# Audio tower on one core: gates and values of the first stage in quarter pieces, folds of the second stage one step later, attention's last stores waited for in the next stage

## The chip, the cores and the metric

The kernel runs on one core of a Trainium2 chip. The metric is the device time of that core in microseconds, the median of three runs. Lower is better. The engines are called TensorE, VectorE, ScalarE, GpSimd and, for issuing transfers, the sync queue (SP). All five run their own instruction lists and meet through semaphores.

## The reference

Everything is fp32. A tokenizer stage reads x, cut into 3000 tokens of 2560 features (32 sequences x 94, the last one of each padded), and a pre-norm transformer block follows:

```python
x = _rms_norm(x, ln_pre_w)
h = jnp.einsum('btd,hd->bth', x, w1)              # 2560 -> 1024
h = jax.nn.silu(h[..., d:]) * h[..., :d]          # gate * value, 512 wide
y = jnp.einsum('btd,od->bto', h, w2)              # 512 -> 1024
h = _rms_norm(y, ln_post_w)
h = h + attention(_layernorm(h))                  # latent q and kv, rope, causal softmax, wo
h = h + ffn(_layernorm(h))                        # base linear + lora experts, router
```

The change lies in the first line of einsum with its gate and value (stage 1), in the second einsum (stage 2), and in the last transfers of attention (stage 3).

## The kernel before

**Stages.** One launch runs five stages one after another: `tok_up` (the first einsum, gate and value), `tok_down` (the second einsum, post-norm, projections to latents, and four "folds" of attention weights per six tiles), `attention`, the output projection `attn_out`, and the feed-forward. Each stage writes one instruction list per engine. The order within an engine is the order in which the code writes it: there is no scheduler. A transfer of the sync queue is issued when all that the queue has to wait for ahead of it is done, so a wait in SP's list holds all later loads.

**Precision.** An fp32 product is made of three fast passes: an operand is split in a high part (ScalarE, line 596: `t_hi`) and the rest (VectorE, line 670: `t_lo`), and TensorE adds lo x hi, hi x lo and hi x hi (lines 734 to 736).

**Stage 1, `tok_up`.** The product of the 1024 x 2560 weights with the tokens is made with seven products of half-size blocks (`SEVEN`) in place of eight. x's tokens are cut in six blocks `TOKC`, four of 512 columns and two of 480; blocks 2pr and 2pr+1 make pair pr of three. Step s of 210 stands for product i = s // 30, pair pr = (s // 10) % 3 and slice kk = s % 10 of ten slices of the inner dimension. Ten steps, a group, fill the four PSUM tiles of one result. In a step
- SP loads one or two pieces of x (line 464) into six slots `raw`, in some steps pieces of the weights (line 450) into six slots `w_raw`. The load of a weight piece waits until the earlier piece of its slot is split (`s_lo_done`);
- GpSimd adds or subtracts two pieces of x (line 538, into `both`), and two of the weights (line 522);
- ScalarE makes `t_hi` (596) and, of the weights, scaled pieces (567) and `s_hi` (579);
- VectorE makes `s_lo` (633), `t_lo` (670), and takes one PSUM tile of the group before into the results `c_t` (`take`, 651 to 655);
- TensorE runs 12 matmuls of 512 or 480 columns, as soon as `t_lo` of the step is there. Operands of five steps have room (`NT`), so VectorE can be at most five steps ahead.

`c_t` holds per token block c a HIGH half (the gates) and a LOW half (the values), each of four quarters m of 128 x 512. The gates are multiplied with the row's norm (line 697, VectorE), go through Silu on ScalarE (line 617) two steps later, and multiply the values (line 702, VectorE). Each is one operation on all four quarters. The tables `GATE_FIRST` and `VALUE` say in which step. Gates stand at steps 163, 166, 169 (c = 0, 2, 4) and 171, 181, 191 (c = 1, 3, 5), values at 176, 186, 196 (c = 1, 3, 5), 199 and 209 (c = 0, 2); c = 4 is done quarter by quarter after the last step. `STORE` sends a finished block to memory as `g_t` (line 470, 1 MB) eight steps later: in the sync queue behind x's loads of steps 184, 194, 204 and 207, and one behind the last.

**Stage 2, `tok_down`.** 24 tiles of 128 tokens. A pipeline of steps (`run_steps`, `stage(k, m, at, ...)`: at a step, the tile that is `at` steps old): g's parts at distance 0, the product y (line 244) at `D_Y` = 1, the latent product a at 3, turned queries at 4. In step 2 (`CENTRE_AT`) the weights of a are centred (line 1102, VectorE) and scaled in eight pieces by ScalarE (`spread`, line 990), and in step 3 `fold_a` multiplies them (line 1234). Four of each six tiles carry one of 16 folds: two TensorE products q (line 1205), copied out by ScalarE (line 1032), then two wide halves v (line 1213), each copied out (line 1005) before the next may use `ps_f`. SP loads a fold's weights two steps ahead of it. A step's code on each engine:

```python
        D_F = 2
                s = fold(k, m, 0)          # SP: the loads
                s = fold(k, m)             # GpSimd, ScalarE, TensorE: at D_F
```

**Stage 3 to 4.** `attention` stores 128 pieces of its output `o_t` (line 1400) from two tiles in turn, and its SP list ends with a wait for all of these stores. Before that it has loaded the first eight slots of the next stage's input. All engines meet at the end of a stage; `attn_out` loads into `raw` (`OutRaw`, object `ox`), and waits for its first `t_lo` (line 1963).

## Time and profile before

| | us |
|---|---|
| median of 3 runs | 2439.2 (2436.16 to 2441.24) |
| profiled execution | 2439.96 |
| its span, first to last instruction | 2438.3 |
| mean granted TensorE clock | 0.982 |
| `tok_up` | 0 to 600 |
| `tok_down` | 600 to 901 |
| `attention` | 901 to 1584 |
| `attn_out` | 1584 to 2065 |
| feed-forward | 2065 to 2438 |

The rows further down are of this one profiled execution. A timeline row gives the start, the duration (us), engine, line, operation, names and shapes, and in brackets how long the engine was idle before and who ended that. A group row adds up all instructions of a line: busy time, mean ns of one, then idle time before them. In the windows, PEclk is the granted TensorE clock as a share of full speed, and DMA the mean busy share of 16 transfer engines. Step numbers of `tok_up` are found by counting `t_lo` operations: step 162 of TensorE begins at 451.44, step 185 loads x at 514.61.

### The profile page before, as it was taken

How to read it: one execution, taken by the hardware profiler on the slowest of the kernel's cores; microseconds unless marked ns; L12 is line 12 of the kernel's file. 1: busy time of each engine (PE TensorE's matmuls, PEld its weight loads, DVE VectorE, ACT ScalarE, POOL GpSimd, SP SyncE). 2: the span in 40 equal slices, each digit the busy share in tenths (PEclk: the TensorE clock that was granted, in tenths of full speed). 3: DMA queues.
4: the chain of work that ended last, by engine and by line, in shares of the span. 5: the costliest groups of instructions: out<-in, count | busy, mean ns of one | idle time of the engine just before them, and what ended most of it. 6: DMA issues, size and time to landing. Idle time of an engine off the chain costs nothing. (4 is left out here: it accounts for less than half of the span.)

```text
span 2438.3 us, 45823 instructions
## 1 busy us (share of the span) xinstructions
PE 2326.4 (95%) x14640; PEld 2038.1 (84%) x14640; DVE 1811.2 (74%) x3542; ACT 1240.9 (51%) x3724; POOL 1218.7 (50%) x1012
## 2 busy tenths in 40 slices
PE   8999999988899979999999999899999998999998
PEld 6888888866577758999999999788888877899998
DVE  8987777776467758989898989655776575777775
ACT  5566554442355549999999999732332223111110
POOL 5667776673023336677767776510676553111110
PEclk9999999999999989999999999899999999999999
DMA  7774567777466740111111112296888988122121
GB/s 247 242 233 147 180 214 255 241 241 273 147 214 229 229 143 17 57 52 47 51 56 51 45 51 68 69 327 195 241 250 238 290 271 270 53 70 70 69 69 52
DMA packets 319400, 382.00 MB, mean 157 GB/s; under 512 B 23680, under 2 KB 227968, under 8 KB 319104
## 3 DMA queue, kind: packets, MB, share of 16 engines
q1 hardware_dynamic: 311472, 352.30, 45.8%
q0 software_dynamic: 7184, 25.69, 2.7%
q10 hardware_dynamic: 576, 2.10, 0.3%
q8 instruction: 64, 1.05, 0.2%
q14 instruction: 104, 0.85, 0.1%
HBM read 297.68 MB, written 81.80 MB: 156 GB/s over the span
## 5 line engine op out<-in xcount | busy, mean ns | idle before, releaser
L1537 ACT ACTIVATE attn_prob<-attn_prob,attn_bias 94x94 f32<-94x94 f32 x1024 | 366.7, 361 | 45.8 <-DVE attn_bias L1613 44.3
L670 DVE TENSOR_TENSOR up_t_lo<-early_raw,up_t_hi 128x512 fp32r<-128x512 f32 (+1 forms) x210 | 221.0, 1056 | 120.1 <-ACT up_t_hi L596 117.8
L538 POOL TENSOR_TENSOR early_raw<-early_raw 128x512 f32<-128x512 f32 (+1 forms) x150 | 231.9, 1551 | 142.5 <-DMA early_raw<-x_f 82.3
L1658 POOL TENSOR_TENSOR attn_prob<-attn_prob,attn_share 94x752 f32<-94x752 f32 x128 | 188.3, 1471 | 177.5 <-DVE attn_share L1621 177.5
L1913 POOL TENSOR_TENSOR early_raw<-early_raw 128x512 f32<-128x512 f32 x120 | 170.2, 1423 | 199.9 <-DMA early_raw<-o_t 199.5
L1963 DVE TENSOR_TENSOR out_t_lo<-early_raw,out_t_hi 128x512 fp32r<-128x512 f32 x168 | 159.6, 954 | 139.5 <-ACT out_t_hi L1927 138.7
L596 ACT ACTIVATE up_t_hi<-early_raw 128x512 fp32r<-128x512 f32 (+1 forms) x210 | 130.4, 622 | 258.2 <-POOL early_raw L538 179.6
L1927 ACT ACTIVATE out_t_hi<-early_raw 128x512 fp32r<-128x512 f32 x168 | 105.0, 631 | 307.6 <-POOL early_raw L1913 155.9
L734 PE MATMUL up_ps<-up_t_lo,early_s_hi 128*128 128x512 f32 (+1 forms) x616 | 241.1, 391 | 12.8 <-DVE up_t_lo L670 12.8
L735 PE MATMUL up_ps<-up_t_hi,early_s_lo 128*128 128x512 f32 (+1 forms) x616 | 239.1, 388 | 0.0
L736 PE MATMUL up_ps<-up_t_hi,early_s_hi 128*128 128x512 f32 (+1 forms) x616 | 238.9, 388 | 0.0
L2117 POOL TENSOR_TENSOR ffn_res<-shared_k_t,ffn_bias 128x1024 f32<-128x1024 f32 x24 | 58.3, 2429 | 303.1 <-DVE ffn_o L2242 263.1
L1537 ACT ACTIVATION_READ_ACCUMULATOR attn_prob<-attn_prob,attn_bias 94x1 f32 x1024 | 192.5, 188 | 0.0
L1986 PE MATMUL out_ps<-early_s_hi,out_t_lo 128*128 128x512 f32 x384 | 150.3, 392 | 9.4 <-DVE out_t_lo L1963 9.4
L1592 DVE TENSOR_TENSOR attn_prob<-attn_ps_s,attn_mask 94x752 f32<-94x752 f32 x128 | 119.3, 932 | 51.9 <-PE attn_ps_s L1452 51.6
L1987 PE MATMUL out_ps<-early_s_lo,out_t_hi 128*128 128x512 f32 x384 | 150.1, 391 | 0.0
L1988 PE MATMUL out_ps<-early_s_hi,out_t_hi 128*128 128x512 f32 x384 | 150.0, 391 | 0.0
L1649 POOL TENSOR_TENSOR attn_q_a<-attn_by_cos,attn_by_sin 64x376 f32<-64x376 f32 x128 | 144.3, 1127 | 10.6 <-POOL attn_by_sin L1645 1.1
L734 PEld LDWEIGHTS up_ps<-up_t_lo,early_s_hi 128*128 128x128 f32 x616 | 116.7, 189 | 38.0 <-issue 8.7
L244 PE MATMUL ffn_ps_o<-ffn_w_hi,ffn_xt_lo 128*128 128x384 f32 (+1 forms) x576 | 138.8, 346 | 1.2 <-DVE ffn_xt_lo L2206 1.2
L736 PEld LDWEIGHTS up_ps<-up_t_hi,early_s_hi 128*128 128x128 f32 x616 | 116.5, 189 | 22.5
L735 PEld LDWEIGHTS up_ps<-up_t_hi,early_s_lo 128*128 128x128 f32 x616 | 116.6, 189 | 21.8
(267 smaller groups left out, 6628.2 us busy)
## 6 DMA issues: line engine op xcount, KB each, us to landing
early_raw<-o_t SPq DMA_DIRECT2D x288, 256.0 KB, 4.9
early_raw<-x_f SPq DMA_DIRECT2D x240, 256.0 KB, 3.9
shared_ring<-w SPq DMA_DIRECT2D x120, 256.0 KB, 4.0
early_raw<-x_f SPq DMA_DIRECT2D x120, 240.0 KB, 4.0
shared_ring<-wvo SPq DMA_DIRECT2D x96, 256.0 KB, 4.9
o_t<-attn_o_t SPq DMA_DIRECT2D x128, 188.0 KB, 1.9
shared_ring<-wo SPq DMA_DIRECT2D x32, 512.0 KB, 6.7
y<-early_raw POOLq DMA_DIRECT2D x24, 512.0 KB, 3.6
```

Of the source, the lines that this page charges most:

```text
L538: nc.gpsimd.tensor_tensor(both[n % 2][:, 0:w], a, b, SEVEN[i].op_b).then_inc(both_done, 1)
L670: nc.vector.tensor_tensor(t_lo[s % NT][:, 0:w], src, t_hi[s % NT][:, 0:w], ALU.subtract).then_inc(lo_done, 1)
L734: nc.tensor.matmul(o, sh, tl, start=(kk == 0), stop=False)
L735: nc.tensor.matmul(o, sl, th, start=False, stop=False)
L736: last = nc.tensor.matmul(o, sh, th, start=False, stop=(kk == KH - 1))
L1537: last = nc.scalar.activation(prob[u % NPR][0:SEQ, h, part], prob[u % NPR][0:SEQ, h, part], ACT.Exp, bias=bias[u % 2][0:SEQ, n:n + 1], sca ...
L1658: nc.gpsimd.tensor_tensor(p4, p4, share[u % 2][0:SEQ, :].unsqueeze(2).broadcast_to((SEQ, 8, SEQ)), ALU.mult).then_inc(prob_done, 1)
L1913: nc.gpsimd.tensor_tensor(ox.at(s), ox.at(s), ox.at(s, 1), ox.product(s).op_a).then_inc(ox.both_done, 1)
L1963: nc.vector.tensor_tensor(t_lo[s % NT][:], ox.at(s), t_hi[s % NT][:], ALU.subtract).then_inc(ox.lo_done, 1)
L1986: nc.tensor.matmul(ps[g % NB][:], t_lo[s % NT][:, j, :], sh, start=(kk == 0), stop=False)
L1987: nc.tensor.matmul(ps[g % NB][:], t_hi[s % NT][:, j, :], sl, start=False, stop=False)
L1988: last = nc.tensor.matmul(ps[g % NB][:], t_hi[s % NT][:, j, :], sh, start=False, stop=(kk == KB - 1))
```

## The change

Three edits, each on its own.

**Quarters.** Gate, Silu and value work on one quarter (`piece(c, mh, m)`, 128 x 512 or 480) instead of the half. Waits on `taken` are for that quarter alone. New tables give a step for each quarter: gates of c = 0 at steps 162 to 165, c = 2 at 166 to 169, c = 1 at 170, 172, 173, 174, c = 4 at 175, 177, 182, 188, c = 3 at 189, 189, 190, 190, c = 5 at 191, 191, 192, 192. Values: c = 1 at 193, 193, 194, 194, c = 3 at 195 to 198, c = 0 at 199, 199, 200, 200, c = 5 at 201, 201, 202, 202, c = 2 four at 209. The stores follow eight steps behind a block's last value as before: 202, 206, 208 and two behind the last load. Lines of the changed file are 12 to 13 higher from the middle of `tok_up` on.

**Folds.** `D_F` = 3 instead of 2, the load of a fold's weights at distance 1 instead of 0. All engines' fold parts move to one step later.

**Attention.** The wait for the last stores of `o_t` leaves the end of attention's SP list and stands at the start of `attn_out`'s SP list. The tiles `o_t` are placed elsewhere in the stage's memory (moved up behind `w_lo`, not shown), and their semaphores belong to `OutRaw`.

```diff
@@ -414,18 +414,27 @@
         STATS = ps[group(4, 2) % 2][0][:, width(2):width(2) + TILES]
         RATE_AT = STAT_AT + KH + 4
         assert RT * len(TOKC) == TOKP and RT == 4 * P
-        GATE_FIRST, VALUE = {}, {}
-        for pr in range(PAIR):
-            GATE_FIRST[RATE_AT + 9 + 3 * pr] = 2 * pr
-            GATE_FIRST[KH * group(5, pr + 2) + 1] = 2 * pr + 1
-            VALUE[KH * group(5, pr + 2) + 6] = 2 * pr + 1
-            if pr < 2:
-                VALUE[KH * group(6, pr + 1) + 9] = 2 * pr
-        gates = sorted(GATE_FIRST, key=lambda s: s)
-        nth_gate = {GATE_FIRST[s]: n for n, s in enumerate(gates)}
-        values = sorted(VALUE)
-        nth_value = {VALUE[s]: n for n, s in enumerate(values)}
-        STORE = {s + 8: VALUE[s] for s in values}
+        G6, G7 = KH * group(5, 0), KH * group(6, 0)
+        GATE_AT = {0: (G6 + 12, G6 + 13, G6 + 14, G6 + 15), 2: (G6 + 16, G6 + 17, G6 + 18, G6 + 19),
+                   1: (G6 + 20, G6 + 22, G6 + 23, G6 + 24), 4: (G6 + 25, G6 + 27, G7 + 2, G7 + 8),
+                   3: (G7 + 9, G7 + 9, G7 + 10, G7 + 10), 5: (G7 + 11, G7 + 11, G7 + 12, G7 + 12)}
+        VALUE_AT = {1: (G7 + 13, G7 + 13, G7 + 14, G7 + 14), 3: (G7 + 15, G7 + 16, G7 + 17, G7 + 18),
+                    0: (G7 + 19, G7 + 19, G7 + 20, G7 + 20), 5: (G7 + 21, G7 + 21, G7 + 22, G7 + 22),
+                    2: (G7 + 29, G7 + 29, G7 + 29, G7 + 29)}
+        gates = sorted((x, c, m) for c in GATE_AT for m, x in enumerate(GATE_AT[c]))
+        values = sorted((x, c, m) for c in VALUE_AT for m, x in enumerate(VALUE_AT[c]))
+        nth_gate = {(c, m): n for n, (x, c, m) in enumerate(gates)}
+        nth_value = {(c, m): n for n, (x, c, m) in enumerate(values)}
+        STORE = {VALUE_AT[c][-1] + 8: c for c in VALUE_AT}
+        assert len(STORE) == len(VALUE_AT) and min(GATE_AT[0]) >= RATE_AT + 8
+        def gates_of(s):
+            return [(c, m) for x, c, m in gates if x == s]
+        def values_of(s):
+            return [(c, m) for x, c, m in values if x == s]
         def rates(c):
@@ -433,11 +442,15 @@
         def rate(c):
             a, w = TOKC[c]
-            return ssq[:, a:a + w].unsqueeze(1).broadcast_to((P, MB, w))
+            return ssq[:, a:a + w]
         def half(c, mh):
             a, w = TOKC[c]
             return c_t[:, MB * mh:MB * mh + MB, a:a + w]
+        def piece(c, mh, m):
+            a, w = TOKC[c]
+            return c_t[:, MB * mh + m, a:a + w]
         @block.sync
         def _(sp):
@@ -466,7 +479,7 @@
             def store(c):
                 a, w = TOKC[c]
-                sp.wait_ge(g_done, nth_value[c] + 1)
+                sp.wait_ge(g_done, nth_value[c, MB - 1] + 1)
                 sp.dma_start(d["g_t"][:, :, a:a + w], half(c, LOW)).then_inc(g_stored, 16)
             sp.dma_start(fac, d["pre_ln"]).then_inc(fac_in, 16)
@@ -495,7 +508,7 @@
                     for n in range(4):
                         ws.load(sp, n)
                 if s == STEPS - 5:
-                    sp.wait_ge(gate_scaled, len(TOKC))
+                    sp.wait_ge(gate_scaled, MB * len(TOKC))
                     sp.dma_start(k_t[:].rearrange("p (n w) -> p n w", n=KM), d["wa"]).then_inc(wa_in, 16)
             for s in sorted(STORE):
                 if s >= STEPS:
@@ -611,10 +624,9 @@
                     nc.scalar.activation(dst, raw[raws.slot(k)][:, 0:w], ACT.Square).then_inc(sq_done, 1)
                 if s in begins:
                     first_piece(begins[s])
-                if s - 2 in GATE_FIRST:
-                    c = GATE_FIRST[s - 2]
-                    act.wait_ge(gate_scaled, nth_gate[c] + 1)
-                    nc.scalar.activation(half(c, HIGH), half(c, HIGH), ACT.Silu).then_inc(silu_done, 1)
+                for c, m in gates_of(s - 2):
+                    act.wait_ge(gate_scaled, nth_gate[c, m] + 1)
+                    nc.scalar.activation(piece(c, HIGH, m), piece(c, HIGH, m), ACT.Silu).then_inc(silu_done, 1)
         @block.vector
         def _(dve):
@@ -689,17 +701,17 @@
                     nc.vector.tensor_scalar(own, var[:, 0, :], RMS_EPS, None, ALU.mult).then_inc(own_done, 1)
                     dve.wait_ge(pad_set, 1)
                     nc.vector.transpose(r_t, r).then_inc(rate_turned, 1)
-                if s in GATE_FIRST:
-                    c = GATE_FIRST[s]
-                    for n in range(TOKC[c][0] // RT, rates(c)):
-                        dve.wait_ge(rate_in[n], 16)
-                    dve.wait_ge(taken, 4 * last_of[(c // 2, HIGH, c % 2)] + 4)
-                    nc.vector.tensor_tensor(half(c, HIGH), half(c, HIGH), rate(c), ALU.mult).then_inc(gate_scaled, 1)
-                if s in VALUE:
-                    c = VALUE[s]
-                    dve.wait_ge(silu_done, nth_gate[c] + 1)
-                    dve.wait_ge(taken, 4 * last_of[(c // 2, LOW, c % 2)] + 4)
-                    nc.vector.tensor_tensor(half(c, LOW), half(c, LOW), half(c, HIGH), ALU.mult).then_inc(g_done, 1)
+                for c, m in gates_of(s):
+                    if m == 0:
+                        for n in range(TOKC[c][0] // RT, rates(c)):
+                            dve.wait_ge(rate_in[n], 16)
+                    dve.wait_ge(taken, 4 * last_of[(c // 2, HIGH, c % 2)] + m + 1)
+                    nc.vector.tensor_tensor(piece(c, HIGH, m), piece(c, HIGH, m), rate(c), ALU.mult).then_inc(gate_scaled, 1)
+                for c, m in values_of(s):
+                    dve.wait_ge(silu_done, nth_gate[c, m] + 1)
+                    dve.wait_ge(taken, 4 * last_of[(c // 2, LOW, c % 2)] + m + 1)
+                    nc.vector.tensor_tensor(piece(c, LOW, m), piece(c, LOW, m), piece(c, HIGH, m),
+                                            ALU.mult).then_inc(g_done, 1)
             g = NI * PAIR
             a, w = TOKC[4]
             for m in range(MB):
@@ -859,20 +871,20 @@
-        D_F = 2
+        D_F = 3
...
                     if not first(t, 2):
                         sp.wait_ge(key_done, t - 1)
                     sp.dma_start(turns[u % 2][:], d["turns"][t]).then_inc(turns_in[u % 2], 16)
-                s = fold(k, m, 0)
+                s = fold(k, m, 1)
                 if s is not None:
                     p, b, turn = s
                     if not first(p, 2):
@@ -1347,7 +1359,7 @@
         prob_t_done = mem.sem("prob_t_done")
         weighed = mem.sem("weighed")
         o_done = mem.sem("o_done")
-        o_stored = mem.sems("o_stored", 2)
+        o_stored = ox.o_stored
         zeroed = mem.sem("zeroed")
         cleared = mem.sem("cleared")
         table_in = mem.sem("table_in")
@@ -1405,8 +1417,6 @@
                     ox.load(sp, m - 4)
             run_steps(sp, N, DEPTH, U, body, last=1)
-            for b in range(2):
-                sp.wait_ge(o_stored[b], 16 * N // 2)
         @block.tensor
         def _(pe):
@@ -1771,6 +1781,7 @@
         self.all = mem.sb("raw", [P, self.SLOTS, 512])
         self.raw = [self.all[:, i, :].rearrange("p (k n) -> p k n", n=P) for i in range(self.SLOTS)]
         self.raw_in = mem.sems("raw_in", self.SLOTS)
+        self.o_stored = mem.sems("o_stored", 2)
         self.both_done = mem.sem("both_done")
         self.lo_done = mem.sem("lo_done")
         self.steps = 2 * self.PAIR * len(OUT_SEVEN)
@@ -1882,6 +1893,8 @@
                 sp.wait_ge(taken, PAIR * final + pr + 1)
                 sp.dma_start(d["h"][t], c_t[t]).then_inc(lent_stored if t == lent else h_stored, 16)
+            for b in range(2):
+                sp.wait_ge(ox.o_stored[b], 16 * PAIRS * GROUPS // 2)
             for s in range(STEPS):
                 i, pr, half = ox.place(s)
                 if s >= ox.SLOTS:
```

In the listings of order below, a row is one instruction (x and a number: so many alike in a row) with its line, its names and its size; the listings of the changed kernel have its own lines.

VectorE in `tok_up`, before: the value of block 1 (line 702, step 176) among `take`, `s_lo` (633) and `t_lo` (670) of steps 176 to 181; the next row is the gate of block 3 (line 697).

```order
L702 TENSOR_TENSOR up_c_t<-up_c_t 128x4x512
L670 TENSOR_TENSOR up_t_lo<-early_raw,up_t_hi 128x480
L655 TENSOR_TENSOR up_c_t<-up_c_t,up_ps_2 128x512
L633 TENSOR_TENSOR early_s_lo<-shared_ring,early_s_hi 128x512
L670 TENSOR_TENSOR up_t_lo<-early_raw,up_t_hi 128x480
L655 TENSOR_TENSOR up_c_t<-up_c_t,up_ps_3 128x512
L633 TENSOR_TENSOR up_s_lo<-shared_ring,up_s_hi 128x512
L670 TENSOR_TENSOR up_t_lo<-early_raw,up_t_hi 128x480
L633 TENSOR_TENSOR up_s_lo<-shared_ring,up_s_hi 128x512
L670 TENSOR_TENSOR up_t_lo<-early_raw,up_t_hi 128x512
L633 TENSOR_TENSOR up_s_lo<-shared_ring,up_s_hi 128x512
L670 TENSOR_TENSOR up_t_lo<-early_raw,up_t_hi 128x512
```

After, the same stretch of VectorE's list: quarters of block 4's gate (line 709) at steps 177 and 182.

```order
L709 TENSOR_TENSOR up_c_t<-up_c_t,shared_k_t 128x480
L645 TENSOR_TENSOR early_s_lo<-shared_ring,early_s_hi 128x512
L682 TENSOR_TENSOR up_t_lo<-early_raw,up_t_hi 128x480
L667 TENSOR_TENSOR up_c_t<-up_c_t,up_ps_3 128x512
L645 TENSOR_TENSOR up_s_lo<-shared_ring,up_s_hi 128x512
L682 TENSOR_TENSOR up_t_lo<-early_raw,up_t_hi 128x480
L645 TENSOR_TENSOR up_s_lo<-shared_ring,up_s_hi 128x512
L682 TENSOR_TENSOR up_t_lo<-early_raw,up_t_hi 128x512
L645 TENSOR_TENSOR up_s_lo<-shared_ring,up_s_hi 128x512
L682 TENSOR_TENSOR up_t_lo<-early_raw,up_t_hi 128x512 x2
L709 TENSOR_TENSOR up_c_t<-up_c_t,shared_k_t 128x480
L645 TENSOR_TENSOR early_s_lo<-shared_ring,early_s_hi 128x512
```

Between steps 176 and 182 stand two quarters in place of two whole operations.

The sync queue at the end of `tok_up`, before: x's loads (464), stores of `g_t` (470), and the next stages' weights (212, 499). The first store of the list stands ahead of x of step 185.

```order
L470 DMA g_t<-up_c_t 512x1x512
L464 DMA early_raw<-x_f 128x512 x20
L470 DMA g_t<-up_c_t 512x1x512
L464 DMA early_raw<-x_f 128x512 x10
L464 DMA early_raw<-x_f 128x480 x2
L212 DMA shared_ring<-w 128x1024 x4
L464 DMA early_raw<-x_f 128x480 x8
L470 DMA g_t<-up_c_t 512x1x480
L464 DMA early_raw<-x_f 128x480 x2
L499 DMA shared_k_t<-wa 128x3072
L464 DMA early_raw<-x_f 128x480 x4
L470 DMA g_t<-up_c_t 512x1x512
```

After (loads 477, stores 483, weights 212 and 512):

```order
L477 DMA early_raw<-x_f 128x512 x30
L477 DMA early_raw<-x_f 128x480 x2
L212 DMA shared_ring<-w 128x1024 x4
L477 DMA early_raw<-x_f 128x480 x4
L483 DMA g_t<-up_c_t 512x1x512
L477 DMA early_raw<-x_f 128x480 x6
L512 DMA shared_k_t<-wa 128x3072
L477 DMA early_raw<-x_f 128x480 x2
L483 DMA g_t<-up_c_t 512x1x512
L477 DMA early_raw<-x_f 128x480 x4
L483 DMA g_t<-up_c_t 512x1x512
L477 DMA early_raw<-x_f 128x480 x2
```

The 32 loads of x and the four of weights follow one another without a store, and three stores stand ahead of the last 14, the last 6 and the last 2 loads of 480 columns.

TensorE in `tok_down` at the steps 2 and 3, before: fold 0 (1205, 1213) behind y of tile 1, then y of tile 2 with fold 1's first product.

```order
L1205 MATMUL down_ps_f<-down_wk,down_wqn 128x128 x2
L1213 MATMUL down_ps_f<-shared_ring,down_wv 64x512 x4
L244 MATMUL down_ps_y<-early_s_hi,down_g_lo 128x512 x2
L244 MATMUL down_ps_y<-early_s_lo,down_g_hi 128x512 x2
L244 MATMUL down_ps_y<-early_s_hi,down_g_hi 128x512 x2
L244 MATMUL down_ps_y<-early_s_hi,down_g_lo 128x512 x2
L244 MATMUL down_ps_y<-early_s_lo,down_g_hi 128x512 x2
L244 MATMUL down_ps_y<-early_s_hi,down_g_hi 128x512 x2
L1205 MATMUL down_ps_f<-down_wk,down_wqn 128x128 x2
```

After: fold 0 (1217, 1225) behind y of tile 2 (the three rows at the top are the end of it), then `fold_a` (1246) and the first a.

```order
L244 MATMUL down_ps_y<-early_s_hi,down_g_lo 128x512 x2
L244 MATMUL down_ps_y<-early_s_lo,down_g_hi 128x512 x2
L244 MATMUL down_ps_y<-early_s_hi,down_g_hi 128x512 x2
L1217 MATMUL down_ps_f<-down_wk,down_wqn 128x128 x2
L1225 MATMUL down_ps_f<-shared_ring,down_wv 64x512 x2
L1246 MATMUL down_ps_a<-shared_k_t,early_raw 128x384 x32
L244 MATMUL down_ps_a<-down_wga_hi,down_g_lo 128x384
L244 MATMUL down_ps_a<-down_wga_lo,down_g_hi 128x384
```

Fold 0 has moved behind y of tile 2, in step 3, and its two wide halves stand on either side of `fold_a` and a of tile 0.

## Rows read from the trace of the kernel before

**Rows 1.** The page's first part: busy us of each engine, share of the span, instructions.

```profile
PE 2326.4 (95%) x14640; PEld 2038.1 (84%) x14640; DVE 1811.2 (74%) x3542; ACT 1240.9 (51%) x3724; POOL 1218.7 (50%) x1012
```

**Rows 2.** Windows: length, busy PE PEld DVE ACT POOL, PEclk, DMA share, GB/s.

```profile
447.00:491.00 44.00, 44.00 (x200) 37.10 (x199) 35.04 (x28) 24.07 (x31) 33.26 (x19) 1.00 0.74 240
491.00:532.00 41.00, 31.81 (x116) 24.24 (x115) 30.18 (x24) 20.09 (x31) 28.22 (x18) 0.88 0.71 232
560.00:584.00 24.00, 24.00 (x110) 20.44 (x109) 8.78 (x10) 4.24 (x7) 9.26 (x8) 1.00 0.95 345
624.00:638.00 14.00, 8.52 (x27) 4.79 (x26) 7.43 (x21) 8.80 (x18) 2.77 (x4) 0.76 0.30 103
```

**Rows 3.** Timeline of TensorE in stage 1, steps 162 and 189.

```profile
451.44 0.39 PE L734 MATMUL up_ps<-up_t_lo,up_s_hi 128*128 128x512 f32 x1
...
525.23 0.79 PE L734 MATMUL up_ps<-up_t_lo,up_s_hi 128*128 128x512 f32 x1 [4.72 <-DVE up_t_lo L670]
```

**Rows 4.** Groups of GpSimd and VectorE, 447 to 569 us.

```profile
L538 POOL TENSOR_TENSOR early_raw<-early_raw 128x512 f32<-128x512 f32 (+1 forms) x41 | 70.0, 1714 | 38.6 <-DVE up_t_lo L670 20.8 <-DMA early_raw<-x_f 17.8
L522 POOL TENSOR_TENSOR shared_ring<-shared_ring 128x512 f32<-128x512 f32 x10 | 15.2, 1516 | 1.4 <-ACT shared_ring L567 1.3
L670 DVE TENSOR_TENSOR up_t_lo<-early_raw,up_t_hi 128x512 fp32r<-128x512 f32 (+1 forms) x40 | 47.0, 1176 | 27.4 <-ACT up_t_hi L596 26.9
L697 DVE TENSOR_TENSOR up_c_t<-up_c_t,shared_k_t 128x2048 f32<-128x2048 f32 (+1 forms) x6 | 16.4, 2737 | 0.0
L702 DVE TENSOR_TENSOR up_c_t<-up_c_t 128x2048 f32<-128x2048 f32 (+1 forms) x4 | 11.1, 2784 | 0.0
```

**Rows 5.** Timeline of VectorE: one earlier step of stage 1, and step 162.

```profile
104.25 1.21 DVE L670 TENSOR_TENSOR up_t_lo<-early_raw,up_t_hi 128x512 fp32r<-128x512 f32 x1
105.38 0.68 DVE L680 TENSOR_TENSOR shared_k_t<-shared_k_t,shared_ring 128x512 f32<-128x512 f32 x1
105.98 0.65 DVE L651 COPY up_c_t<-up_ps 128x480 f32<-128x480 f32 x1
106.55 1.22 DVE L670 TENSOR_TENSOR up_t_lo<-early_raw,up_t_hi 128x512 fp32r<-128x512 f32 x1
...
446.24 0.69 DVE L670 TENSOR_TENSOR up_t_lo<-early_raw,up_t_hi 128x512 fp32r<-128x512 f32 x1 [0.15 <-ACT up_t_hi L596]
```

**Rows 6.** Timelines of GpSimd and sync queue, and the queue's waits 447 to 569.

```profile
522.14 1.26 POOL L538 TENSOR_TENSOR early_raw<-early_raw 128x512 f32<-128x512 f32 x1 [6.28 <-DMA early_raw<-x_f]
523.36 1.27 POOL L522 TENSOR_TENSOR shared_ring<-shared_ring 128x512 f32<-128x512 f32 x1
...
513.89 0.68 SPq L470 DMA_DIRECT2D g_t<-up_c_t  x1
...
SPq L450 <- DVE early_s_lo L633: 15.8, 4, 6.6
```

**Rows 7.** Timelines of ScalarE, TensorE and VectorE at stage 2's first fold.

```profile
624.92 4.14 ACT L990 ACTIVATE shared_k_t<-shared_k_t,down_post_col 128x384 f32<-128x384 f32 x8
628.96 1.00 ACT L1048 ACTIVATE down_junk<-down_ps_y 128x1024 bf16<-128x1024 f32 x1
...
631.32 1.15 ACT L1059 ACTIVATE early_raw<-down_z,down_vec 128x1024 f32<-128x1024 f32 x1 [0.45 <-DVEq L1145]
...
630.92 1.97 PE L1213 MATMUL down_ps_f<-shared_ring,down_wv 128*64 128x512 f32 x4 [4.76 <-ACT down_wv_out L1005]
...
625.76 1.21 DVE L1135 TENSOR_TENSOR down_z<-down_ps_y,down_post 128x1024 f32<-128x1024 f32 x1
```

**Rows 8.** Timeline of TensorE at the end of stage 2.

```profile
888.17 0.52 PE L1287 MATMUL down_ps_d<-all_ident,down_qk 128*128 128x128 f32 x3 [2.59 <-POOL down_qk L966]
```

**Rows 9.** Timelines of the sync queue and TensorE at attention's end.

```profile
1558.97 23.35 SPq L1400 DMA_DIRECT2D o_t<-attn_o_t  x9
1584.31 0.34 SPq L1877 DMA_DIRECT2D out_c_t<-y  x1
...
1585.75 0.80 PE L1986 MATMUL out_ps<-early_s_hi,out_t_lo 128*128 128x512 f32 x1 [6.75 <-DVE out_t_lo L1963]
```

4 lines of the change are left out of this document (2 added, 2 removed).

## The prediction

> **What bounds the kernel now.** I read the busy shares first: TensorE works 2326.4 of 2438.3 us [rows 1], so the time is TensorE's work plus the 112 us in which it stands, and a change is worth what it takes from those. The windows then say where it stands near the places the change touches. In the first stage it is full until 491, then busy 31.81 of 41 us up to 532, at a mean granted clock of 0.88 [rows 2]. That is 9.2 us of waiting, and 0.12 x 41 = 4.9 us (4.7 without the part that fell into waits) of matmuls at the lower of the two clock levels (1.2 instead of 2.4 GHz); the clock fell after TensorE had stood, as 4.72 us before 525 [rows 3]. Together 13.9 us. In the second stage's start, from 624 to 638, it is busy 8.52 of 14 us at a clock of 0.76: 5.5 us of waiting and 0.24 x 14 = 3.3 us of slow clock [rows 2].
>
> Why it stands at 491 to 532 takes three views. From 447 to 569 (steps 162 to 202) VectorE and GpSimd have nearly the same list of SBUF work to do. A GpSimd add takes 1.22 us when it starts alone (522.14 to 523.36, [rows 6]) and 1.71 in the mean [rows 4]; the t_lo subtraction takes 0.69 alone, or 1.21 when a GpSimd add is running [rows 5]. The two take turns, so their times add up. 51 adds x 1.22 = 62 us; 50 splits (t_lo and s_lo) x 0.60, the distance at which one follows another (105.38 to 105.98 in the pattern of [rows 5]: 2.30 a step holds one add of 1.22, half-hidden, a split, a one-tile operation and a copy) = 30; ten big gates and values x 2.2 = 22. Sum 114 of the 122 us. Into the 8 us left fall the waits of the sync queue: it stood 15.8 us for s_lo [rows 6], and at 513.89 put a 1 MB store of g_t ahead of the loads of x, for which GpSimd then stood 6.28 us [rows 6]. TensorE has to have these 40 steps in 40 x 2.72 = 109 us; it had a lead of 451.44 - 446.93 = 4.5 us at step 162 [rows 3, 5], used it, and stood.
>
> **The change, part by part.**
>
> *Quarters.* Eleven VectorE operations of about 2.75 us (16.4 us for six, 11.1 for four, [rows 4], one later) become 44 of 512 columns, the six Silus 24. Their sum hardly moves: four quarters at the 0.60 pitch are 2.4 us against 2.2, ten sets +2 us. On ScalarE, busy 24.07 of 44 and 20.09 of 41 us [rows 2], the 18 more instructions lie beside other work. So the port floor of steps 162 to 202 is 114 + 2 = 116 us, less the lead of 4.5, against 109: TensorE must still give 2.5 to 3.5 us if nothing overlaps beyond the pitches, none if a few per cent more of it does. What is gained is place: before step 185, where weights are folded on nearly each step, stand 15 quarters instead of six whole operations (24 quarters). Nine quarters x 0.6 to 1.0 = 5.4 to 9 us leave the stretch in which the lead was zero. They come back at steps 188 to 202, with 25 quarters in 15 steps; a step with one such operation and a copy runs in 2.30 us [rows 5], under TensorE's 2.72, one with two in about 2.9, a little over. Ten double steps cost 2 us of lead, the five single ones give 2 back.
>
> *Stores.* The store that stood at step 184 goes to 202, the others to 206, 208 and behind the last load. That frees 1.05 MB / 345 GB/s [rows 2] = 3.0 us in front of x at step 185, and removes most of the 6.28 us of GpSimd. But between steps 202 and 209 now three stores lie ahead of the last load of x instead of two. There the queues are full already (share 0.95, 345 GB/s from 560 to 584, [rows 2]). The extra 1.1 MB are 3.2 us. Since the heavy stretch before is shorter, SP comes to these loads earlier; I charge half, 1.5 us, bounds 0 and 3.2.
>
> Sum of the stage: of 13.9 us I leave 3 for the port floor, 2 for the chain over s_lo that the change does not touch (sync queue to DMA to GpSimd to ScalarE to VectorE), 1.5 for the last loads: **7.4 us gained**. Bounds: 13.9 (all gone) and 0 (the port floor and the stores take it all).
>
> A rule of the Trainium skill speaks against quarters. The trace shows the cost of a short operation as a pitch of 0.60 us in a row of them [rows 5]. The page "VectorE: DVE Perf Modes", section "The TRN2 errata — SBUF-src ops pay a fixed extra latency per instruction", gives an fp32 tensor_tensor (N+151)/0.96 ns, which is 691 ns for 512 columns and 2291 for 2048. By it four quarters would cost 0.47 us more than one whole, ten sets 4.7 us instead of my 2, and the stage would gain 4.7 instead of 7.4 us. The duration of a single one agrees (0.69); the pitch does not, and the sum goes by the pitch.
>
> *Folds.* The distance from load to use stays two steps; both move by one. At step 2 TensorE stood 4.76 us before the second half of fold 0 [rows 7], because ScalarE, between the fold's first and second copy, had to spread eight pieces (4.14 us) and square y [rows 7]. After the change TensorE goes on with y of tile 2 (24 matmuls x 0.23 = 5.5 us, its g_lo is there) up to 629.3 and the fold's first product up to 629.9. ScalarE spreads from 622.5 on, begins y's square when z is there (625.76 + 1.21 = 627.0), needs 631.32 + 1.15 - 628.96 = 3.5 us for y [rows 7], and with the next g_hi and the fold's own copies (1.3 us) is done at 631.9. So TensorE waits 2.1 us where it waited 5.5, and after so little idle I expect no slow clock: 5.5 + 3.3 - 2.1 = **6.7 us gained**; with the slow clock back, 3.4. At the other end the last fold falls to step 25, where TensorE stood 2.59 us for GpSimd [rows 8]: the fold's 2.7 us of matmuls fill that hole and push the last tile by some 2.5 us, while a fold less stands before. That is nil, plus or minus 1. SP is moved past one load of g (tile 2 is loaded ahead of fold 1 now), which only helps. Nothing in the steady part changes.
>
> *Attention's stores.* The last store is issued until 1558.97 + 23.35 = 1582.32, the next stage begins on SP at 1584.31, TensorE at 1585.75 [rows 9]. The 2.0 us between are landing plus the engines' meeting. How they split no row shows; I take 0.4 us for the meeting, which stays, and 1.6 for the landing, since a landing is the longer of the two: **1.6 us gained**, bounds 0 and 2.0. SP itself waits as before, with eight slots of o_t (22 us of matmuls) loaded ahead and nothing else queued behind it but y and weights needed from step 3 and 6 on: at nothing.
>
> Total 7.4 + 6.7 + 1.6 = 15.7 us. The profiled execution took 2439.96 us (span 2438.3), 0.8 over the median of 2439.2: 2439.96 - 15.7 = **2424.3 us**.
>
> **The rivals.**
> 1. *All stalls of the first stage go*: the floor overlaps and the late stores hide. For it: t_lo takes 1176 ns in the mean against 690 alone [rows 4, 5], so operations do run side by side for a part. Against: the pitches hold that part already. 13.9 + 6.7 + 1.6 = 22.2: 2417.8.
> 2. *The stage gains nothing*: VectorE and GpSimd do the same work, the double steps and the stores at the end take back what the place gives. For it the floor of 116 us and share 0.95 at the end; against, the 6.28 us behind one store. 6.7 + 1.6 = 8.3: 2431.7.
> 3. *The fold's wait only moves*: TensorE stands for the fold's first copy as long as it did for the second, and the clock falls. Stage two gains 1: 7.4 + 1 + 1.6 = 10: 2430.
> 4. *Slower: every quarter waits for a GpSimd add.* Stretched from 0.60 to 1.67 us (0.60 and most of an add of 1.22), 40 quarters cost 67 us instead of the 27.5 of [rows 4]: 39 more. VectorE's idle time in the stretch, 27.4 us before t_lo [rows 4], covers as much; 12 us come on top of today's stalls, and 5 of slow clock: 17 - 8.3 = 8.7 slower, 2448.7. It decides where the mean quarter passes (27.5 + 27.4)/40 = 1.37 us. Against it: there are only 51 adds, and each can hold up one operation.
> That the change does not do what it says is open only for attention: if another engine comes last to the meeting, 1.6 less.
>
> **How the numbers follow.** Forecast 0.45 (2419 to 2429), rival 1 0.15, rival 2 0.22, rival 3 0.11, rival 4 0.07. The range of 8 in 10 leaves out most of rival 4 and the far ends of 1: 2416 to 2435. A measurement of this kernel tells about 0.2%, 4.9 us, from no change: under 2434.3 is faster. The forecast and rival 1 lie under it, of rivals 2 and 3 three quarters (their other ends, a slow clock or stores at 3.2 us, cross it): 0.45 + 0.15 + 0.25 = 0.85; within 0.2% 0.09, slower 0.06.
>
> **What would show it.** Right: no TensorE idle over 1.5 us between 447 and 560 and a granted clock of 0.95 or more there; x's loads at step 185 not behind a store; a wait of about 2 us before fold 0's first wide product with the clock at full speed until the stage's end; TensorE's first product of the output stage about 5.2 us after attention's last instead of 6.75. Wrong: TensorE waiting on t_lo in steps 189 to 194 with VectorE busy throughout (the port), or in 205 to 209 with GpSimd waiting on x (the stores), or the half clock in the second stage's first 15 us beyond its start.

## The result, and the profile after

The changed kernel took 2426.31 us, median of 6 runs (2420.08 to 2427.83), beside 2437.18 for the kernel before in 6 runs. The ratio is 0.9948 with a 95% interval of 0.9937 to 0.9959: faster by 12.7 us (10.0 to 15.4). (The two medians themselves differ by 10.9 us; "less" goes by the ratio everywhere below.) Measured again in the experiments below it was 0.9936 (0.9921 to 0.9951), faster by 15.6 us. The forecast was 15.7 us less and the range 2416 to 2435. The profiled execution took 2427.59 us, its span is 2425.9.

The first part of the page answers to [rows 1]. TensorE's busy time is the same to 0.5 us, so of the 12.4 us between the two spans 11.9 are time in which it stands no longer. Matmuls at the slow clock count as busy for longer: what the first stage got back of that (3.4 us, by the measure further down) came in again elsewhere, 1.9 us of it in the second stage.

```profile
PE 2325.9 (96%) x14640; PEld 2038.6 (84%) x14640; DVE 1821.9 (75%) x3575; ACT 1242.8 (51%) x3742; POOL 1205.4 (50%) x1012
```

The windows of [rows 2], now of the changed kernel (length, busy PE, PEld, DVE, ACT, POOL, granted clock, DMA share, GB/s):

```profile
447.00:491.00 44.00, 44.00 (x199) 37.00 (x198) 41.39 (x40) 25.94 (x44) 30.43 (x21) 1.00 0.78 251
491.00:532.00 41.00, 37.86 (x160) 30.34 (x159) 33.08 (x31) 20.74 (x35) 28.48 (x20) 0.96 0.77 250
560.00:584.00 24.00, 23.79 (x109) 19.83 (x107) 12.57 (x17) 5.38 (x9) 11.97 (x9) 1.00 1.01 388
624.00:638.00 14.00, 12.48 (x41) 6.95 (x40) 7.66 (x25) 5.56 (x13) 2.30 (x4) 1.00 0.39 129
```

Between 491 and 532 TensorE is busy 37.86 us instead of 31.81, at a clock of 0.96 instead of 0.88; 44 matmuls more stand in the window. Between 624 and 638 it is busy 12.48 instead of 8.52, at full clock. What is left of [rows 3] between 491 and 532 is in the main one wait, before step 185 as then. (Counted by `t_lo` operations, the row with 4.72 us in [rows 3] is step 185 too, not 189 as its heading has it.)

```profile
514.01 0.50 PE L746 MATMUL up_ps<-up_t_lo,up_s_hi 128*128 128x512 f32 x1 [0.35 <-DVE up_t_lo L682]
519.52 0.79 PE L746 MATMUL up_ps<-up_t_lo,up_s_hi 128*128 128x512 f32 x1 [2.50 <-DVE up_t_lo L682]
```

The groups of VectorE and GpSimd, 449 to 566 us, answer to [rows 4]:

```profile
L682 DVE TENSOR_TENSOR up_t_lo<-early_raw,up_t_hi 128x512 fp32r<-128x512 f32 (+1 forms) x41 | 42.0, 1026 | 10.4 <-ACT up_t_hi L609 9.7
L709 DVE TENSOR_TENSOR up_c_t<-up_c_t,shared_k_t 128x512 f32<-128x512 f32 (+1 forms) x24 | 29.8, 1255 | 0.0
L713 DVE TENSOR_TENSOR up_c_t<-up_c_t 128x512 f32<-128x512 f32 (+1 forms) x16 | 16.7, 1070 | 0.0
...
L551 POOL TENSOR_TENSOR early_raw<-early_raw 128x512 f32<-128x512 f32 (+1 forms) x41 | 59.3, 1449 | 44.1 <-DVE up_t_lo L682 26.1 <-DMA early_raw<-x_f 11.5 <-issue 6.5
```

A quarter of a gate takes 1255 ns in the mean and of a value 1070, where a quarter of the whole was 684 to 696. The 40 quarters are busy 46.5 us instead of 27.5. In return t_lo fell from 1176 to 1026 ns and GpSimd's adds from 1714 to 1449. Whether this comes of the portions or of the new steps the pair of traces cannot tell; the runs under "Size or place" do.

For the account I worked out of each trace the time from a stage's first matmul to its last, the gap to the next stage, and of TensorE's slow clock the sum of (1 - granted clock) x 2 us over windows of 2 us. These are worked out from the timelines, not rows of a view. The last of them also counts slow clock in which TensorE stood, so it is not all time lost. Of this one profiled pair:

| us | before | changed | difference | forecast |
|---|---|---|---|---|
| start to first matmul | 8.7 | 10.0 | +1.3 | 0 |
| `tok_up` | 587.2 | 579.6 | -7.6 | -7.4 |
| gap | 9.6 | 9.9 | +0.2 | 0 |
| `tok_down` | 290.9 | 287.8 | -3.1 | -6.7 |
| `attention` | 678.6 | 679.8 | +1.2 | 0 |
| gap behind attention | 6.75 | 3.18 | -3.6 | -1.6 |
| `attn_out` and feed-forward | | | -0.8 | 0 |

The sum is -12.4. Two of the forecast's differences do not fit, `tok_down` by 3.6 us and the gap by 2.0 the other way, and for both the experiments have more traces of the same code. The change touches neither the start nor the work within `attention`; over fourteen traces these two range from 8.7 to 11.0 and from 677.8 to 680.4 us, so their differences are chance.

### The profile page after: what moved, and what is told of

Its sections match the earlier page's. It is cut to its first block and busy times, and to the rows that moved or that the text cites. A ratio compares the mean times of both kernels' runs of the same rounds, so it can differ in the third digit from the quotient of the medians.

```text
span 2425.9 us, 45879 instructions
## 1 busy us (share of the span) xinstructions
PE 2325.9 (96%) x14640; PEld 2038.6 (84%) x14640; DVE 1821.9 (75%) x3575; ACT 1242.8 (51%) x3742; POOL 1205.4 (50%) x1012
## 5 line engine op out<-in xcount | busy, mean ns | idle before, releaser
L682 DVE TENSOR_TENSOR up_t_lo<-early_raw,up_t_hi 128x512 fp32r<-128x512 f32 (+1 forms) x210 | 224.0, 1070 | 102.1 <-ACT up_t_hi L609 99.7
L551 POOL TENSOR_TENSOR early_raw<-early_raw 128x512 f32<-128x512 f32 (+1 forms) x150 | 220.2, 1471 | 148.8 <-DMA early_raw<-x_f 72.6
L748 PEld LDWEIGHTS up_ps<-up_t_hi,early_s_hi 128*128 128x128 f32 x616 | 116.0, 188 | 22.4
L244 PE MATMUL ffn_ps_o<-ffn_w_lo,ffn_xt_hi 128*128 128x384 f32 (+1 forms) x576 | 134.8, 339 | 0.0
```

The lines of the kernel that those rows point to most:

```text
L244: last = nc.tensor.matmul(o, x, w, start=a, stop=b, skip_group_check=onto)
L551: nc.gpsimd.tensor_tensor(both[n % 2][:, 0:w], a, b, SEVEN[i].op_b).then_inc(both_done, 1)
L682: nc.vector.tensor_tensor(t_lo[s % NT][:, 0:w], src, t_hi[s % NT][:, 0:w], ALU.subtract).then_inc(lo_done, 1)
L748: last = nc.tensor.matmul(o, sh, th, start=False, stop=(kk == KH - 1))
```

## The experiments

Each kernel was timed in five rounds or more beside the kernel before, four kernels together on one chip. "Less" is against the kernel before, worked out from the ratio and its median there (2438.28, 2437.98 and 2438.48 us for the three sets).

### Each part alone

The three edits were applied to the kernel before one by one. Together they are exactly the changed kernel.

The folds:

```diff
-        D_F = 2
+        D_F = 3
...
-                s = fold(k, m, 0)
+                s = fold(k, m, 1)
```

> Only the fold's step is moved (D_F = 3, loads at distance 1); nothing is left out. Prediction: 6.7 us less than before, nearly all in the first 15 us of the second product's stage, with no half clock there. Rival: the changed kernel's trace shows only 3.2 us less between TensorE's first and last matmul of the stage (290.9 before, 287.8 after), because 2.68 us of waiting with half clock stand at 680 where 1.1 us stood before, and the clock falls earlier at the stage's end; then this run gains about 3 us and shows both places.

Measured: ratio 0.996 (0.9947 to 0.9973), 9.8 us less. `tok_down` took 283.4 us, 7.5 less. Of the wait at the first fold 1.16 us are left, and a new one is there, at 689.58, with the clock at 0.56 to 0.58 for four us:

```profile
689.58 1.97 PE L1213 MATMUL down_ps_f<-shared_ring,down_wv 128*64 128x512 f32 x4 [2.61 <-ACT down_wv_out L1005]
```

The changed kernel has it at the same step. So one of the two places that the rival named showed, and its 3 us did not. At the stage's end the two traces differ, though both have nearly the same waits: here TensorE waits 1.67 us before the last fold and keeps its clock,

```profile
876.88 0.68 PE L1205 MATMUL down_ps_f<-down_wk,down_wqn 128*128 128x128 f32 x4 [1.67 <-ACT down_wv_out L1005]
```

```profile
874.00:886.00 12.00, 8.83 (x46) 5.58 (x42) 5.86 (x29) 7.08 (x26) 4.77 (x13) 1.00 0.36 137
```

there it waits 1.77 and the 12 us around it run at 0.72 (timeline, and window of the changed kernel):

```profile
870.46 0.86 PE L1217 MATMUL down_ps_f<-down_wk,down_wqn 128*128 128x128 f32 x4 [1.77 <-ACT down_wv_out L1017]
```

```profile
868.00:880.00 12.00, 9.52 (x36) 6.17 (x35) 4.17 (x23) 5.89 (x21) 3.96 (x9) 0.72 0.36 137
```

The slow clock takes 3.6 us of the stage in one and 9.1 in the other. The 7.5 us of this trace lie within the interval of the 9.8 (6.6 to 12.9), and the trace has other stages that are shorter without a change in them (`attn_out` 461.1 against 464.8).

Attention's stores:

```diff
-            for b in range(2):
-                sp.wait_ge(o_stored[b], 16 * N // 2)
...
+            for b in range(2):
+                sp.wait_ge(ox.o_stored[b], 16 * PAIRS * GROUPS // 2)
```

> Only the wait for attention's last stores is moved; nothing is left out. Prediction: 1.6 us less. The changed kernel's trace has 3.6 us less between attention's last matmul and the next stage's first (6.75 to 3.18), of which 2.3 us is that the last copy of o_t waited 0.70 instead of 2.99 us for an older store: if that belongs to the change, this run gains 3.6 us and its last copy waits under 1 us; if it was chance, 1.3 to 1.6 us and the copy waits differently from run to run.

Measured: 0.9989 (0.998 to 0.9998), 2.7 us less (0.5 to 4.9). The gap behind attention was 3.01 us. In five traces that wait at the old place (the kernel with the folds alone and four more below) it was 4.66, 4.62, 4.66, 4.42 and 5.01; the 6.75 of [rows 9] is the odd one. Its reason stands on VectorE, where the last copy of o_t waited 2.99 us for the landing of an older store; in the changed kernel it waited 0.70:

```profile
1581.41 0.55 DVE L1584 COPY attn_o_t<-attn_ps_o 128x376 f32<-128x376 f32 x1 [2.99 <-DMA o_t<-attn_o_t]
```

```profile
1571.49 0.55 DVE L1594 COPY attn_o_t<-attn_ps_o 128x376 f32<-128x376 f32 x1 [0.70 <-DMA o_t<-attn_o_t]
```

In eight traces with the wait moved the gap is 2.84 to 5.05 with a median of 3.17. Medians differ by 1.5 us. The two of about 5 (4.93 and 5.05) are just those in which the last copy waited for an older store, as in the kernel before; here one of them, the changed kernel with a copy moved (below):

```profile
1564.62 0.55 DVE L1594 COPY attn_o_t<-attn_ps_o 128x376 f32<-128x376 f32 x1 [2.79 <-DMA o_t<-attn_o_t]
```

So the late landing comes from execution to execution, in 3 of 14 traces and on either side of the change. Like with like, the gap falls from 6.75 to 5.0 with it, and from 4.7 to 3.1 in the mean without it.

The first stage's part alone, all of the change in `tok_up`:

> Only the first stage's part: quarters, their new steps, and the stores that follow them; nothing is left out. Prediction: 7.4 us less. The changed kernel's trace gives 8.8 us between step 162 and the stage's last matmul (144.4 before, 135.6 after). If the three parts add up, this, the fold and the store runs sum to the 12.7 us of the whole change (0.52% of 2437).

Measured: 0.9965 (0.9952 to 0.9978), 8.5 us less. `tok_up` took 582.7 us in this trace. The kernel before and its two variants with the same first stage have 587.2, 587.6 and 587.5; five traces with the changed first stage have 579.6, 578.4, 582.7, 579.1 and 581.5, a mean of 580.3: 7.2 us less. Of these about 3.3 are waits (9.7 to 6.4) and 4.8 slow clock (5.1 to 0.3), minus what the windows overlap.

### Size or place

The quarters, but each block's four in the step in which the whole operation stood:

```diff
-        GATE_AT = {0: (G6 + 12, G6 + 13, G6 + 14, G6 + 15), 2: (G6 + 16, G6 + 17, G6 + 18, G6 + 19),
...
+        GATE_AT = {0: (163, 163, 163, 163), 2: (166, 166, 166, 166), 4: (169, 169, 169, 169),
+                   1: (171, 171, 171, 171), 3: (181, 181, 181, 181), 5: (191, 191, 191, 191)}
+        VALUE_AT = {1: (176, 176, 176, 176), 3: (186, 186, 186, 186), 5: (196, 196, 196, 196),
+                    0: (199, 199, 199, 199), 2: (209, 209, 209, 209)}
```

> The gates and values in quarters, but all four quarters of a block in the step in which the whole operation stood, and the stores behind the same loads as before; nothing is left out. My theory (place, not size): the 13.9 us of stalls and slow clock between 491 and 532 stay, the time is within 2 us of before, 0 to 2 us slower for 33 more operations. Rival (size): GpSimd's adds and the t_lo of the next step come in between the quarters, x is summed sooner, and over half of the first stage's gain (4.4 us or more) is there already.

Measured: 1.0007 (0.9998 to 1.0016), no gain. `tok_up` took 591.0 us, 3.6 more than before. The waits are more, 13.2 us over the stage where it was 9.3 to 10.0, and less of them takes the clock down, 3.4 us instead of 5.1 (timeline of TensorE):

```profile
506.91 0.50 PE L742 MATMUL up_ps<-up_t_lo,early_s_hi 128*128 128x512 f32 x1 [1.85 <-DVE up_t_lo L678]
...
516.59 0.80 PE L742 MATMUL up_ps<-up_t_lo,early_s_hi 128*128 128x512 f32 x1 [3.25 <-DVE up_t_lo L678]
529.22 0.50 PE L742 MATMUL up_ps<-up_t_lo,up_s_hi 128*128 128x512 f32 x1 [2.61 <-DVE up_t_lo L678]
```

Size alone gains nothing. Its price on VectorE is plain here, where steps and stores are those of before (groups, 447 to 569 us, beside [rows 4]):

```profile
L705 DVE TENSOR_TENSOR up_c_t<-up_c_t,shared_k_t 128x512 f32<-128x512 f32 (+1 forms) x24 | 25.2, 1106 | 0.0
L709 DVE TENSOR_TENSOR up_c_t<-up_c_t 128x512 f32<-128x512 f32 (+1 forms) x16 | 14.1, 938 | 0.0
```

The 40 quarters are busy 39.3 us where the ten whole ones were 27.5, and t_lo falls from 1176 to 1039 ns and GpSimd's adds from 1714 to 1459, nearly as far as in the changed kernel. With whole operations at the new steps (the next run) t_lo takes 1234 ns and an add 1679. So it is the portions that shift the waiting from t_lo and the adds to the gates and values.

The whole operations at the changed kernel's steps, each where its last quarter is done:

```diff
-        for pr in range(PAIR):
-            GATE_FIRST[RATE_AT + 9 + 3 * pr] = 2 * pr
...
+        GATE_FIRST = {165: 0, 169: 2, 174: 1, 188: 4, 190: 3, 192: 5}
+        VALUE = {194: 1, 198: 3, 200: 0, 202: 5, 209: 2}
```

> The kernel before, with each whole gate and value moved to the step in which the changed kernel does its last quarter (gates at 165, 169, 174, 188, 190, 192, values at 194, 198, 200, 202, 209), and its stores eight steps on, as in the changed kernel; nothing is left out. So the place without the size. Quarters at the old steps gave nothing (stage 591.0 us against 587.4). Theory (place alone): the first stage takes 580.3 us as with quarters, 7 us less than before. Rival (place and size together): three or four whole operations of 2.75 us fall into steps 188 to 194 one per two steps, hold up t_lo there, and TensorE, whose lead is 2 us at 188, stands: less than 4 us gained.

Measured: 0.9972 (0.9962 to 0.9982), 6.8 us less (4.4 to 9.3). `tok_up` took 581.7 us, 5.7 less than before and 1.4 more than the mean with quarters, but inside the five's spread (578.4 to 582.7). The rival's "less than 4" is out: place, with the stores that follow it, brings 80% of the gain or more.

And of place, the stores alone: gates and values stay, only the stores of g_t go behind later loads.

```diff
-        STORE = {s + 8: VALUE[s] for s in values}
+        STORE = {202: 1, 206: 3, 208: 0, 210: 5, 217: 2}
```

> The kernel before with its gates and values as they were, but its stores of g_t behind x's loads of steps 202, 206, 208 and two behind the last load, as in the changed kernel; nothing is left out. My sum had the store ahead of step 185's x as most of the 6.28 us for which GpSimd stood. Theory: that wait falls by 2 to 3 us (the landing of this x took 7.5 us behind the store, 5.6 in the changed kernel), TensorE's 4.72 us before step 185 with it and 1 to 2 us of half clock; the stage is 3 us shorter or more. Rival: the x is late since the queue stood for s_lo, not for the store: under 1 us; or the third store before the last x takes it back at steps 206 to 208.

Measured: 0.9979 (0.9967 to 0.999), 5.1 us less (2.4 to 8.0). `tok_up` took 582.7 us, 4.7 less. The timelines of the sync queue, GpSimd and TensorE at step 185 answer to [rows 3] and [rows 6]:

```profile
514.88 0.80 SPq L450 DMA_DIRECT2D shared_ring<-w  x2
515.73 13.81 SPq L464 DMA_DIRECT2D early_raw<-x_f  x14
...
520.76 1.29 POOL L538 TENSOR_TENSOR early_raw<-early_raw 128x512 f32<-128x512 f32 x1 [3.06 <-DMA early_raw<-x_f]
...
523.90 0.50 PE L734 MATMUL up_ps<-up_t_lo,up_s_hi 128*128 128x512 f32 x1 [0.61 <-DVE up_t_lo L670]
```

From the issue of x to GpSimd's add are 5.0 us, where it was 7.5 before (514.61 to the 522.14 of [rows 6]), and GpSimd stands 3.06 us instead of 6.28. The theory holds, and it holds with more than its 3 us. The queue still comes to this x only at 515.73, behind weights for which it stood for s_lo. The edit moves four stores, and only the first stood ahead of step 185.

Over the whole stage it looks like two thirds of the gain for the stores, but the sum hides two parts that work against each other. I cut the stage in three, by the steps at which TensorE begins (worked out from the timelines):

| us | before (3 traces) | stores late (1) | and whole operations moved (1) | changed (5 traces) |
|---|---|---|---|---|
| to step 162 | 442.5 (442.2 to 442.8) | 443.2 | 443.3 | 443.2 (442.3 to 444.0) |
| steps 162 to 190 | 90.4 (90.3 to 90.5) | 86.1 | 80.8 | 80.6 (79.4 to 82.4) |
| step 190 to the end | 54.5 (54.0 to 54.8) | 53.4 | 57.6 | 56.5 (54.9 to 57.2) |

In the heavy stretch the stores bring 4.3 us, the place of gates and values another 5.3, and their quartering nothing beyond the spread. Behind it the late stores alone cost nothing, but the stage that comes there sooner loses 2.0 us again in the mean. There TensorE waits 1.0 to 1.1 us in the last two steps in all five traces, where it was 0.1 before the change, and in four of them 1.1 to 1.5 us in the six steps ahead of those, where it was 0 to 0.8. GpSimd's adds stand for the loads of x at that place before the change and behind it (2.2 to 5.9 us each between 570 and 582, in the first trace of before and in the second one of the changed kernel), so that the loads set the pace there; that this is why the gain is lost again is argued, not tested.

### The ends of the argument: s_lo and the last stores

The changed kernel with the weights loaded behind the next step's x:

```diff
-                if s in begins:
+                if s in begins and s < 160:
                     load_weights(begins[s])
+                if s - 1 in begins and s - 1 >= 160:
+                    load_weights(begins[s - 1])
```

> The changed kernel, but from step 160 on the sync queue issues a step's weight loads behind x of the next step; nothing is left out. In the changed kernel the queue stands 13.4 us for s_lo ahead of such loads, with the next x behind them, and TensorE still stands 2.50 us before step 185 with 2 us of half clock. Theory (the chain over s_lo holds x): 2 to 4 us less than the changed kernel, no wait over 1 us left between 490 and 530. Rival (VectorE and GpSimd's port is full there): x comes sooner, but the wait only moves, under 1 us less; or the weights come late and TensorE waits for s_lo from step 180 on, up to 3 us more.

Measured: 0.993 (0.9914 to 0.9946), 17.1 us less than before, where the changed kernel measured beside it has 15.6. The medians differ by less than their intervals. In the trace the wait of 2.50 us is gone, the longest between 490 and 560 is this (TensorE),

```profile
510.78 0.50 PE L748 MATMUL up_ps<-up_t_lo,up_s_hi 128*128 128x512 f32 x1 [0.60 <-DVE up_t_lo L684]
```

and `tok_up` took 577.8 us, 2.5 less than the mean of the changed one. Steps 162 to 190 took 78.3 us, under all five traces without this edit. The queue still stands 12.1 us for s_lo, where it was 13.4.

The changed kernel with all stores of g_t behind the last load of x:

```diff
-        STORE = {VALUE_AT[c][-1] + 8: c for c in VALUE_AT}
+        STORE = {212 + n: c for n, c in enumerate((1, 3, 0, 5, 2))}
```

> The changed kernel with all five stores of g_t behind the last load of x; nothing is left out. I charged 1.5 us (0 to 3.2) for three stores among the last loads. If that is there, TensorE's waits at steps 201 to 208 shrink and the stage is 1 to 2 us shorter; but the g_t stores, 5 MB, then have to land behind it, where the second stage reads g_t from tile 3 on: if they are late there, the second stage gets longer by more than the first gains (5.2 MB at 345 GB/s are 15 us).

Measured: 0.9953 (0.9939 to 0.9967), 11.5 us less than before. `tok_up` took 576.5 us, 3.8 less than the mean. Of these, 1.3 stand in the last two steps, which took 5.4 us where all five traces have 6.6 to 6.7: that is what the stores among the last loads cost, near the 1.5 that I charged. The other 2.5 are no more than traces of equal code differ by. But the second stage's first product comes 12.31 us behind the first stage's last, not 9.85:

```profile
598.56 1.22 PE L244 MATMUL down_ps_y<-early_s_hi,down_g_lo 128*128 128x512 f32 x2 [12.31 <-DVE down_g_lo L1129]
```

It gains nothing against the changed kernel (11.5 us beside 12.7 and 15.6).

### Do the parts add up, and the new wait of the folds

Alone the parts gave 9.8 + 2.7 + 8.5 = 21 us, the whole 12.7. The changed kernel was measured again, and beside it with the fold's edit undone (`D_F` = 2 and the loads at distance 0, all else as changed).

> The changed kernel itself once more, beside the kernel before and the three kernels of this call, since its parts alone gave 9.8 + 2.7 + 8.5 = 21 us where the whole gave 12.7. In its first trace the half clock took 11.2 us of the second stage, 4.4 of them at its step 24 to 25 after a wait of 1.77 us; the kernel with the fold's edit alone had the same wait (1.67) there without a half clock. If that fall of the clock is chance from execution to execution, this run lies between 12 and 20 us under before and its trace may lack it. If the parts really stand in each other's way, it stays at 12 to 13 us and the half clock is there again.

Measured: 0.9936 (0.9921 to 0.9951), 15.6 us less. `tok_down` took 283.7 us, with 3.6 us of slow clock (9.1 in the first trace by the same measure, which does not bear out the 11.2 of the text above). The half clock behind the last fold is there but short (window 864 to 876):

```profile
864.00:876.00 12.00, 9.19 (x40) 5.95 (x39) 5.34 (x26) 5.66 (x23) 4.39 (x11) 0.86 0.35 137
```

At step 6 the clock did not fall at all. TensorE waited 1.11 and 1.37 us before the two wide halves there instead of 2.68 at once, at full clock:

```profile
674.00:686.00 12.00, 9.52 (x47) 6.77 (x47) 8.04 (x29) 7.29 (x20) 3.50 (x9) 1.00 0.29 89
```

With the clock down at one place less this execution's stage is 4.1 us shorter than the first one's, of the same code, so the shortfall against the 21 us is no sign that the parts stand in each other's way.

> The changed kernel with the fold's edit undone (D_F = 2, loads at distance 0); nothing is left out. If the parts add up: 8.5 + 2.7 = 11.2 us under before. If the fold is worth less beside the other parts, this run is as fast as the whole or within 3 us of it (12.7 under before).

Measured: 0.9958 (0.9943 to 0.9974), 10.2 us less, near the 11.2 of the two parts alone. So the fold is worth 5.4 us beside the others. From the traces: seven with the fold at two steps have `tok_down` at 290.6 to 291.4, mean 291.0; five with it at three steps 283.4, 283.7, 287.3, 287.7 and 287.8, mean 286.0. The difference is 5.0 us. The five lie in two clusters 4 us apart, which go with the slow clock: 3.6 us in the two shorter ones, 8.8 to 9.1 in the others, at nearly equal waits (16.8 to 17.6 us, 22.4 in the mean before). The three long ones have the clock fall both at step 6 and behind the last fold, the two short ones at one of these places. With two steps the slow clock takes 7.1 to 9.2 us, so in the mean the fold's gain is waits, 5.1 us, and hardly clock. Sum by traces: 7.2 + 5.0 + 1.5 = 13.7 us, between the two measurements of the whole. I take the 21 as the error of three differences, each uncertain by 2 to 3 us.

The new wait. In the changed kernel's first trace, timelines of VectorE, ScalarE and TensorE at step 6:

```profile
678.97 0.69 DVE L1129 TENSOR_TENSOR down_g_lo<-down_g_raw,down_g_hi 128x512 fp32r<-128x512 f32 x1 [1.97 <-issue]
679.58 1.22 DVE L1147 TENSOR_TENSOR down_z<-down_ps_y,down_post 128x1024 f32<-128x1024 f32 x1
...
680.89 1.02 ACT L1060 ACTIVATE down_junk<-down_ps_y 128x1024 bf16<-128x1024 f32 x1 [4.04 <-DVE down_z L1147]
...
682.34 0.58 ACT L1017 ACTIVATE down_wv_out<-down_ps_f 128x512 f32<-128x512 f32 x1
...
682.97 1.89 PE L1225 MATMUL down_ps_f<-shared_ring,down_wv 128*64 128x512 f32 x4 [2.68 <-ACT down_wv_out L1017]
```

At the head of the loop VectorE stands 1.97 us for nothing that the profile shows (1.7 to 2.0 in the seven traces with the fold at three steps, 2.6 to 2.9 in those with two). g_lo, z, ScalarE's square and then its copy of the fold follow one another, and TensorE waits for the last. The copy needs none of the others. So it was put first:

```diff
+                if f is not None:
+                    fold_half(f, 0)
                 s = stage(k, m, D_Y, U, TILES)
...
                                          bias=own[:, bass.ds(t, 1)]).then_inc(yroot_done, 1)
-                if f is not None:
-                    fold_half(f, 0)
```

> The changed kernel, but ScalarE copies the fold's first wide half out of PSUM before it squares y, not after; nothing is left out. In the changed kernel's trace TensorE stands 2.68 us at 680.29 for this copy (start 682.34) which stands behind the square of y (680.89), which stands behind z and a 1.97 us issue gap of VectorE, and the clock falls. Theory: with the copy first it can start at 678, the wait and its half clock are gone: 3 to 4 us less than the changed kernel. Rival: the copy now waits for TensorE's product behind y and holds the square up by about 1 us in each of 16 folds, the chain over y becomes late, and the run is as fast as the changed kernel or slower.

Measured: 0.9911 (0.9895 to 0.9927), 21.7 us less than before and 6.1 less than the changed kernel measured beside it. `tok_down` took 277.3 us. The groups of TensorE, 600 to 890, of the changed kernel measured again and of this one (idle before, with its releasers, is the last part):

```profile
L1225 PE MATMUL down_ps_f<-shared_ring,down_wv 128*64 128x512 f32 x128 | 35.4, 632 | 10.2 <-ACT down_wv_out L1017 5.4 <-ACT down_wq_out L1044 4.0
```

```profile
L1225 PE MATMUL down_ps_f<-shared_ring,down_wv 128*64 128x512 f32 x128 | 34.5, 618 | 2.8 <-ACT down_wq_out L1044 2.8
L1217 PE MATMUL down_ps_f<-down_wk,down_wqn 128*128 128x128 f32 x64 | 10.3, 284 | 4.0 <-ACT down_wv_out L1017 3.9
```

The waits of the wide halves fell from 10.2 to 2.8 us: with the one at 680 went those of 0.7 to 1 us that came once in six tiles. The narrow products wait 4.0 us in place of 1.8. Over the stage the waits fell from 17.3 to 12.1 us. The rival (y late by 1 us in each fold) did not show.

Both mends in the changed kernel:

> The changed kernel with ScalarE's first fold copy ahead of the square, and the weight loads from step 160 on behind x of the next step; nothing is left out. The copy alone gave 21.7 us under before, against 15.6 for the changed kernel in the same call, and its second stage 277.3 us against 283.7 to 287.8; the weights alone 17.1. If they add up: 23 us under before; the first stage 578 to 580 us, the second 277.

Measured: 2414.93 us, ratio 0.9905 (0.989 to 0.9919), 23.2 us less than before, the fastest of all. `tok_up` took 575.2 us, and the window that began this study is nearly full:

```profile
491.00:532.00 41.00, 40.24 (x177) 32.76 (x177) 39.39 (x35) 22.55 (x38) 30.41 (x21) 1.00 0.75 253
```

`tok_down` took 280.5 us where the copy alone had 277.3, at waits no longer (11.6 us against 12.1). The difference goes with the clock behind the last fold, after waits of 2.07 and 2.06 us (the copy alone first, then both):

```profile
864.52 0.68 PE L1217 MATMUL down_ps_f<-down_wk,down_wqn 128*128 128x128 f32 x4 [2.07 <-ACT down_wv_out L1017]
862.00:874.00 12.00, 8.07 (x42) 5.51 (x43) 5.69 (x28) 7.11 (x26) 5.13 (x14) 1.00 0.35 137
...
859.80 0.68 PE L1219 MATMUL down_ps_f<-down_wk,down_wqn 128*128 128x128 f32 x4 [2.06 <-ACT down_wv_out L1019]
857.00:869.00 12.00, 9.22 (x35) 5.78 (x34) 4.17 (x22) 5.90 (x20) 3.96 (x9) 0.72 0.36 137
```

Against the copy alone the ratio's interval does not tell a gain.

## Why the prediction was right, and where it was not

The forecast of 15.7 us less lies just outside the first interval (10.0 to 15.4) and inside the second (11.9 to 19.3), its time of 2424.3 between the two medians 2426.31 and 2422.58. That the time came so near in the first measurement is partly luck: the sum started from one execution of 2439.96 us, 2.8 above the median of before measured there, and the gain was 3.0 too large; the two cancel to 2.0. By its own steps:

- **First stage, 7.4.** Measured 7.2. The point said that what is gained is place, with nine quarters of 5.4 to 9 us leaving the heavy stretch and 3.0 us for the store. The runs give 5.3 and 4.3 there, so the mechanism was right; the store was sized by its bandwidth and was worth 1.3 more. As a sum, 13.9 less 3 and 2 is 8.9 us for steps 162 to 190, measured 9.9.
- **Quarters cost +2 us.** This took them at 0.60 us each, so that "their sum hardly moves". It moves: at the old steps a quarter took 0.98 us in the mean (39.3 us for 40), in the changed kernel 1.16. TensorE felt little of it: at the old steps the stage was 3.6 us longer in one trace, and the whole 1.7 us slower (0.5 us faster to 3.9 slower). By the Trainium skill's page "VectorE: DVE Perf Modes", in its section on the errata of SBUF operations, it would have been 4.7 us, which is an estimate from its durations and lies outside that interval. The 2 lie inside, but not for the reason given, and a single operation's 0.69 us, which agrees with the page, is no measure of one that stands beside GpSimd's adds.
- **Last loads, 1.5 (0 to 3.2).** From step 190 on the stage lost 2.0 us in the mean. With the stores away from there the last two steps were 1.3 us shorter, but this cannot be had, since the second stage then starts 2.5 us later and the whole is no faster.
- **Chain over s_lo, 2.** 2.3 us in steps 162 to 190 in one trace, when the weights went behind x.
- **Folds, 6.7.** Measured 5.0. The first fold went as worked out: TensorE waited 1.52 us where I had 2.1, and the clock was full. "Nothing in the steady part changes" was the step that failed: the fold at the loop's head (step 6) now waits 2.4 to 2.7 us, and the clock falls there in four of five traces; and at the end, where I had nil, a fold that waits 1.7 to 1.8 us takes the clock down in four of five. So of the 3.3 us of slow clock that the sum counted as gained 1.2 are there in the mean (8.0 to 6.8). A saving that I had not counted goes the other way: the waits at the later folds, 7.1 us in the trace of before, are 4.2 in that of the changed kernel. Of rival 3, the wait only moves, 1.7 us came true, at another place than it named.
- **Attention's stores, 1.6.** Measured 1.5 between medians of the gap. The trace of before was misleading by 2.1 us in this place, which neither helped nor hurt, since the sum took the wait's part alone. The signal that I gave, 5.2 instead of 6.75, would have come only with the late landing (4.93 and 5.05 in two traces); without it the gap went from 4.7 to 3.1.
- **The signs.** Of those for "right", the clock of 0.95 or more between 491 and 532 came (0.96), and x of step 185 behind no store. The idle time under 1.5 us did not: 2.50 us stood before step 185. The wait before fold 0 came, but not the full clock up to the stage's end. The sign for the stores, TensorE waiting in the last steps with GpSimd standing for x, showed too, with 1.0 us in the changed kernel's first trace.
- **Rival 4, every quarter waits for an add.** A quarter took 46.5 / 40 = 1.16 us in the mean, under the 1.37 at which it would have decided, and nearer to it than to the 0.60 of my pitch. What I had missed is that the other operations become shorter by it.

## What to carry to other kernels

A wait is dear when it takes the clock with it: look for the one transfer or copy that is queued ahead of what the busiest engine needs, beside counting the work on the other engines; in the stretch studied here each of the two was worth 4 to 5 us. Cut a stage where its limit changes before sharing out its gain: over the whole stage the moved gates and values looked like 1 us, since what they gave in one part was mostly lost in the next. When an operation moves to another step, write down for each engine what stands ahead of it there, also at a loop's head; the wait that came back here was one copy behind a square that it did not need. And size a term on several traces of the same code, since one trace had a gap 2 us too long and stages of equal code differed by 4 us.

## What the runs showed of the hardware

The granted clock does not follow from the length of the wait alone. Behind the last fold of the second stage, with waits of 1.67, 1.77 and 1.77 us, it was 1.00, 0.86 and 0.72 over 12 us in three executions; with waits of 2.07 and 2.06 us it was 1.00 and 0.72, and the stage 277.3 and 280.5 us long. In the first stage 2.27 us of standing left the clock full in one execution and 1.91 us took it down in another.

VectorE stood 1.7 to 2.9 us at the head of the second stage's loop without any releaser in the profile, in all 14 traces.

A GpSimd add and a VectorE operation on SBUF stretch each other (t_lo 0.69 us alone, about 1.2 beside an add, [rows 5]). With the same work in smaller portions at the same steps, VectorE's gates and values rose from 27.5 to 39.3 us of busy time, and its t_lo and GpSimd's adds of x became shorter, from 1176 to 1039 ns and from 1714 to 1459.
